# The third part of the split messages moves from VectorE to GpSimd, and five quads of buckets are split in place of three

## The reference

```python
h = relu(layernorm(x)); x = x + hgnn(h)          # two hyperbolic layers, each with
                                                 # agg = segment_sum(xt[src] * w, dst)
h = relu(layernorm(x))
m = relu(concat(h[src], h[dst]) @ W1 + b1)       # 128 hidden features, per edge and self loop
e = m @ W2 + b2
x = x + segment_sum(e, dst) / max(counts, 1)
```

## Time and profile before

| | |
|---|---|
| median of 3 runs | 1223.57 us (1220.88 to 1223.95) |
| the profiled execution's own time | 1225.43 us |
| its span, first to last instruction | 1223.6 us |
| mean granted TensorE clock | 0.950 |
| busy over the span | PE 87%, DVE 82%, ACT 55%, POOL 2% |
| message stage, groups at their steady pace | about 730 us to 1212 us of the span |

### The profile page before, as it was taken

One profiled execution on the slowest core, in us unless ns is written; L12 is line 12 of the kernel. 1 busy time (PEld: TensorE's weight loads), 2 busy tenths in 40 slices (PEclk: granted clock), 3 DMA queues, 4 the chain that ended last, 5 costly groups with the idle time before them and its releaser, 6 DMA issues.

```text
span 1223.6 us, 53479 instructions
## 1 busy us (share of the span) xinstructions
PE 1063.2 (87%) x21956; PEld 984.6 (80%) x21956; DVE 1001.1 (82%) x1477; ACT 669.2 (55%) x1837; POOL 27.5 (2%) x28
## 2 busy tenths in 40 slices
PE   2079989898898988559999579999999999999997
PEld 2057877777777777358999559999999999999997
DVE  8789999999999997465554868888888888888884
ACT  5348888888888887300001475555555555555552
POOL 7000000000000000100000000000000000000000
PEclk9579999999999999769999679999999999999999
DMA  2003232222323223439991244444444445444440
GB/s 79 0 32 124 92 122 99 115 118 96 122 92 122 108 106 123 183 140 372 354 371 35 86 149 159 157 156 156 156 156 156 156 157 158 157 158 155 159 149 29
DMA packets 45160, 171.75 MB, mean 140 GB/s; under 512 B 19472, under 2 KB 19798, under 8 KB 45115
## 3 DMA queue, kind: packets, MB, share of 16 engines
q1 hardware_dynamic: 45115, 171.12, 39.2%
HBM read 122.95 MB, written 48.14 MB: 140 GB/s over the span
## 4 chain that ended last, share of the span: by engine, by line
PE 53%; DVE 32%; issue 8%; DVEq 4%; ACT 3%; DMA 0%; POOL 0%; POOLq 0%; ACTq 0%
PE PS L1475 17%; PE PS L1477 11%; DVE arena L985 8%; PE PS L1495 7%; PE PS L1354 7%; DVE arena L962 5%; PE PS L1490 5%; DVE arena L970 4%; DVE arena L948 3%; PE PS L1382 3%; DVE arena L957 2%; DVEq L344 2%; PE PS L1430 1%; DVE Cw L777 1%; DVE rows L777 1%
## 5 line engine op out<-in xcount | busy, mean ns | idle before, releaser
L1475 PE MATMUL PS<-arena 125*128 125x128 bf16 x3600 | 344.9, 219 | 6.3 <-ACT RT L714 6.2
L1475 PEld LDWEIGHTS PS<-arena 125*128 125x128 bf16 x3600 | 250.6, 97 | 11.2 <-issue 7.3
L1354 PE MATMUL PS<-arena,A 125*64 125x72 f32 x4800 | 178.1, 229 | 69.1 <-DVE aggTw L996 40.2
L1354 PEld LDWEIGHTS PS<-arena,A 125*64 125x64 f32 x4800 | 164.4, 138 | 78.7 <-DVE A L866 27.0
L609 ACT ACTIVATE arena<-arena 128x72 bf16<-128x72 bf16 x864 | 216.9, 343 | 2.1 <-DVE arena L970 2.1
L728 ACT ACTIVATE arena<-PS 128x512 bf16<-128x512 f32 (+2 forms) x336 | 172.2, 543 | 82.6 <-PE PS L1477 82.5
L721 ACT ACTIVATE arena<-arena 128x512 bf16<-128x512 f32 x144 | 90.9, 631 | 153.8 <-DVE arena L1198 153.7
L1477 PE MATMUL PS<-arena 108*128 108x128 bf16 x1200 | 167.6, 221 | 0.0
L1477 PE MATMUL PS<-arena,HTw 108*128 108x128 bf16 x1200 | 165.8, 219 | 0.0
L1339 PE MATMUL PS<-arena 128*128 128x72 bf16 x3600 | 126.9, 199 | 0.0
L1339 PEld LDWEIGHTS PS<-arena 128*128 128x128 bf16 x3600 | 120.8, 101 | 4.9
(11 more groups left out here) (188 smaller groups left out, 1458.3 us busy)
## 6 DMA issues: line engine op xcount, KB each, us to landing
adjacency<-arena SPq DMA_DIRECT2D x48, 900.0 KB, 3.6
arena<-adjacency SPq DMA_DIRECT2D x48, 900.0 KB, 4.8
Bw<-slot_rows SPq DMA_DIRECT2D x48, 800.0 KB, 4.1
Cw<-slot_rows SPq DMA_DIRECT2D x48, 700.0 KB, 4.4
arena<-q_table SPq DMA_DIRECT2D x144, 18.0 KB
q_table<-arena SPq DMA_DIRECT2D x6, 336.0 KB
slot_rows<-slot_row SPq DMA_DIRECT2D x49, 13.0 KB
x_sb<-in_x SPq DMA_DIRECT2D x1, 700.0 KB
```

The costliest lines, as they stand in the source:

```text
L1354: last = mm(sums[half, :], A[:, b, :], adjacency[0:PN, b, :], start=(b < 2), stop=(b >= NB - 2))
L1475: mm(ps, OTs[k][:, b, :], P3[:, b, part, :], start=(part == 0), stop=False)
```

## The change

Five quads are split in place of three, so 20 of 25 buckets go through the three bf16 parts and 5 stay in f32. The subtraction for the third part (`low`) leaves VectorE and becomes a loop of GpSimd's own, five instructions per group. In VectorE's step the five `rest` instructions stand behind `source_onehots`, with the two destination one-hots behind the first and the second of them, and `sum_onehots` behind the last. The two buffers of the window of Q (`qs`) move to a part of the arena that another path of the kernel uses, which makes room for the larger `H3`.

```diff
-SPLIT = (0, 1, 2)
+SPLIT = (0, 1, 2, 3, 4)
...
-        qs = [carve(HID, bf16, HR).rearrange("p (a h) -> p a h", h=HID) for _ in range(2)]
+        qs = [arena[0:HR, early - GT * HID * 2 + (25 + i) * HID:early - GT * HID * 2 + (26 + i) * HID].bitcast(bf16)
+              .rearrange("p (a h) -> p a h", h=HID) for i in range(2)]
...
+            def low(g, k, q):
+                i, at_b = split_slot(q)
+                pool.wait_ge(s_mid_set, nth(len(SPLIT) * g + i))
+                nc.gpsimd.tensor_tensor(H3[k][:, at_b, 2, :], Hs[k][:, 4 * q:4 * q + 4, :], H3[k][:, at_b, 1, :],
+                                        ALU.subtract).then_inc(s_low_set, 1)
+
+            def low_parts(g, k):
+                pool.wait_ge(s_sum_done, nth(g - 2))
+                for q in SPLIT:
+                    low(g, k, q)
+
+            with pool.If(fast == 1):
+                turns(pool, low_parts)
...
-            def low(g, k, q):
-                i, at_b = split_slot(q)
-                ve.wait_ge(s_mid_set, nth(len(SPLIT) * g + i))
-                nc.vector.tensor_tensor(H3[k][:, at_b, 2, :], Hs[k][:, 4 * q:4 * q + 4, :], H3[k][:, at_b, 1, :],
-                                        ALU.subtract).then_inc(s_low_set, 1)
-
...
-                rest(g, k, SPLIT[0])
-                if ahead:
-                    destination_onehots(1 - k, 0)
-                low(g, k, SPLIT[0])
-                rest(g, k, SPLIT[1])
-                if ahead:
-                    destination_onehots(1 - k, 1).then_inc(s_spread_set, 1)
-                low(g, k, SPLIT[1])
-                rest(g, k, SPLIT[2])
+                for q in SPLIT:
+                    rest(g, k, q)
+                    if ahead and q < 2:
+                        last = destination_onehots(1 - k, q)
+                    if ahead and q == 1:
+                        last.then_inc(s_spread_set, 1)
                 if ahead:
                     sum_onehots(g + 1, 1 - k)
-                low(g, k, SPLIT[2])
```

## The result

The changed kernel takes 1215.74 us (median of 6 runs, 1212.62 to 1217.30) against 1223.76 us before; the ratio is 0.9931 with a 95% interval of 0.9917 to 0.9944. It is faster by 0.7%. The forecast was 1233.6 us, and slower had a chance of 0.61. The fast rival had 0.29; its time was 1208.5 us.

A forecast was written before the change was run, and what follows sets the result against it. TensorE bounds the kernel; the VectorE-GpSimd loop would replace it at 10.45 us. Seven groups gain 2.2, 40 lose 12.8, last sums give back 0.6: +10.0, so 1233.6 us; range 1207 to 1272, forecast's own 1227 to 1252.

The forecast's parts named there:

- The fast rival: TensorE stays the bound because low is cheap or the turns fit; 1208.5 us, chance 0.29.
- the walk through one group: VectorE and GpSimd operations laid in order from the second destination one-hots' end, taking turns; period 10.45 us.
- point between gain and loss, 10.22: Group period from about which down the fast case, TensorE as the bound, was to decide.
- My sum said 1.35: Wait from rest 2 to rest 4 on ScalarE: 0.63 + 0.59 + two hops, 1.35 us.
- The 0.14 that holding saves: An operation held by the other engine was to need 0.14 us less after release; low 1.06, not 1.20.
- TensorE's gain: 32 f32 records out, 24 bf16 matmuls in: 0.31 us less a group, so 9.82 us.
- The cover: Second destination one-hots end 4.1 us before `spread` wants them; used up at 0.63 per group in 7 groups.
- VectorE's count: VectorE's own work a group, 8.26 - 0.89 = 7.37 us, by count no bound.
- low at 1.20 us fresh: GpSimd's subtraction of 512 elements, in proportion to a two-input row of 850 in 1.99 us: 1.20 us.
- that rival: `rest` on VectorE takes turns with GpSimd too: period 12.7 us, 1340 us, chance 0.04.
- GpSimd's operation wasn't dear: Rival in which GpSimd's low costs 1.42 us: period 11.5 us, 1285 us, chance 0.12.

The follow-up runs named there:

- the one-column kernel: The changed kernel, but from the third group on GpSimd subtracts one column of each bucket's third part in place of 128; ratio to before 0.9901.
- The spare subtraction: The changed kernel with one more GpSimd subtraction of 128 columns on a spare tile in front of low 0; 1232.47 us, ratio to before 1.0064.
- the four-quad kernel: The changed kernel with four quads split (16 of 25 buckets) in place of five, low on GpSimd; ratio to before 0.9951.
- the kernel with the one-hots first: The changed kernel with the two one-hots of the sums in front of rest 4; ratio to before 0.9910.
- three kernels with different loops: The changed kernel with one column of the third part (0.9901), sums' one-hots before rest 4 (0.9910), or quad 4's low on VectorE (0.9926).

## Why the prediction was wrong

The step that failed is the walk through one group, "With a hop more I take 10.45 us". The mechanism was right: the turns of VectorE and GpSimd form a loop that outlasts TensorE's work. But the loop was sized at 10.45 us and measured 9.99, 0.46 us less, and the forecast's own point between gain and loss, 10.22, lay only 0.23 us below the forecast period. Ends of each step from the end of the second destination one-hots, as forecast and as the timelines above have them (910.13 taken off):

| step | forecast (us) | measured (us) |
|---|---|---|
| rest 4 ends | 2.60 | 2.47 |
| `OB` starts, ends | 2.65, 3.50 | 2.38, 3.28 |
| low 3 ends | 4.56 | 4.30 |
| `Os` ends | 4.90 | 4.69 |
| low 4 ends | 5.96 | 5.71 |
| source one-hots end | 6.86 | 6.56 |
| rest 0 ends | 7.46 | 7.16 |
| first destination one-hots end | 8.42 | 8.12 |
| low 0 ends | 9.48 | 9.14 |
| second destination one-hots end | 10.38 | 9.98 |
| with the hop | 10.45 | |

The order of the turns is the forecast one at every step. Where the 0.46 us come from:

- About half is the start of rest 4, forecast at 2.00 and measured at 1.78 (0.22). Rest 4 waits for `middle` and `relu` on ScalarE. I had laid their 0.63 and 0.59 us end to end and allowed 0.13 for two hops (the time from the end of an instruction on one engine to the start of the one that waits for it on another). But `relu` starts 0.10 us before `middle` ends, an overlap that I had read for VectorE and not applied to ScalarE, and each hop took 0.03 us:

```profile
910.76 0.63 ACT L736 ACTIVATE arena<-arena 128x512 bf16<-128x512 f32 x1 [0.76 <-DVE arena L1213]
911.29 0.58 ACT L743 ACTIVATE arena<-PS 128x512 bf16<-128x512 f32 x1
```

From the end of rest 2 (910.73) to the start of rest 4 (911.91) are 1.18 us. My sum said 1.35, and the walk had rounded that up to 1.40.

- A low that has been held takes 1.02 us, not 1.06, three times in the loop: 0.12. The 0.14 that holding saves was right. A low with nothing in its way takes 1.16 us (911.47 to 912.63), not 1.20.
- The two one-hots of VectorE that are held end 0.85 and 0.84 us after their release, not 0.90: 0.11.
- `Os` ends 0.39 us after low 3, where I had 0.34: this takes 0.05 back.
- The allowance of 0.07 for a hop at the end wasn't there. The five terms add up to 0.47; the rest is rounding.

I also had `OB` wait for the end of low 2. It started 1.04 us into that low, 0.11 before its end, and wasn't held: it took 0.90 us, like the 0.91 us without GpSimd's work in the one-column kernel. This changed nothing in the sum, since rest 4 was forecast to end at the same moment. This account is read from the timelines; no run varied these terms one by one. The small terms all lay on the long side but one, and together they are twice the margin. The spare subtraction shows that a loop of 10.41 us does make the kernel slower.

Two smaller errors of the prediction stand beside this one.

- TensorE's gain is 10.155 - 9.92 = 0.23 us a group, not 0.31. The 20 f32 records take 0.78 us, not 0.68: by the line that the four-quad kernel bore out, a run of them has a fixed part of 0.155 us and 31 ns for each record, and I had spread the fixed part over the records. With 0.31 the fast rival's 1208.5 was too low; the one-column kernel, where TensorE is the bound, has 1212.07, 12.4 us less than the kernel before on its chip, where 15 had been forecast.
- The cover was not 4.1 us. At the second steady group L1196 ended at 739.33, and the sums in front of `spread` ended at 741.15. With the 0.3 us that pass between the end of L1196 and `spread`, 1.5 us were left. One wait of 1.59 us in front of the source one-hots (at 755.75) took most of it. The row of that wait names L1482, but the last `spread` that these one-hots need had ended by 748.33, where the sums behind it start. The load of the destinations, issued at 749.48, took 6.1 us to land, where the median of this load in these groups is 4.5, so it landed just before the one-hots started:

```profile
Cw<-slot_rows SPq DMA_DIRECT2D x1, 700.0 KB, 6.1
```

The chain shows the two regimes:

```profile
807.84 1.95 PE PS L1495 x60
...
817.75 1.95 PE PS L1495 x60
```

Up to here the period is TensorE's 9.91; over the 36 groups from 827.77 on it is 9.992, the loop's.

What held: VectorE's count (the one-column kernel has 299.20 us busy in 400, 7.42 a group, against 7.37); low at 1.20 us fresh (1.16 for low 2; low 0 takes 1.24, of which 0.22 under L1196); that `tensor_scalar` and GpSimd take turns and `rest` doesn't (0.68 against 0.69), so that rival is out, and GpSimd's operation wasn't dear, though mixed in type. By the Trainium skill, page SBUF — State Buffer, section Who interferes with whom, an instruction with at most one SBUF input outside the 2-port modes doesn't contend; `rest`, with one input from PSUM, agrees (0.68 us here, 0.69 before). For `OB`, two SBUF inputs under a running low, the section has it contend. Started 0.22 us into a low it did (1.71 us in the kernel with the one-hots first); started 1.04 us into one it didn't (0.90 us).

## What to carry to other kernels

When two engines take turns, walk one group in order and use the spacing of starts for every engine in it, not the durations; then give the period an error as wide as the sum of the small allowances, and compare this with the margin to the other engine's period. Work moved to a slower engine can pay although it holds up the faster one: here 1.44 us on GpSimd replaced 0.60 on VectorE and the loop still became 0.30 us shorter, because of GpSimd's 7.2 us a group (5 x 1.443) only 2.0 held VectorE up (0.71 on L1192, 0.96 on L1206, 0.30 on the two L1196, against their means in the one-column kernel). Once the loop is below the bound engine's need, shortening it further gives nothing: three kernels with different loops have TensorE's 9.92.

## What the runs showed of the hardware

- A GpSimd subtraction of 128x512 (f32 minus bf16 to bf16) held VectorE's `tensor_scalar` for 1.02 us after being let in itself; one of 4 elements a partition took 0.25 us and held nothing that could be seen (L1208 0.53, destination one-hots 1.04).
- An instruction that was held ends sooner after its release than its own duration: 0.85 us for 1.05 (L1192, L1196), 1.02 for a low that takes 1.16 with nothing in its way.
- A bf16 `tensor_tensor` of VectorE with two SBUF inputs (128x1440) was held when it started 0.22 us into a low (1.71 us) and not when it started 1.04 us into one (0.90).
- A run of f32 matmuls (weights of 128 rows and 64 columns, 72 moving columns, at a granted clock of 1.00) took 0.78 us for 20 records, 1.28 for 36 and 1.78 for 52, which a line of 0.155 us and 31 ns a record fits.
